# Attention outputs moved by DMA into the transposed layout and scaled on GpSimd, and the row maxima turned by one transpose of 48 columns

## The reference, cut to what matters

```python
# attn_a, causal
attn = where(causal, einsum('bhqd,bhkd->bhqk', q, k) * scale, -inf)
a = clip(attn, -100, 100); m = max(a, -1); e = exp(a - m)
p = e / (sum(e, -1) + 1e-6)
p = p + 1e-8
p = p / sum(p, -1)
out = einsum('bhqk,bhkd->bhqd', p, v)      # then @ w_proj, + x
# ffn, attention part (src is reshaped: 8 batches of 512 rows in this kernel)
probs = softmax(scores, -1)
attn = einsum('bhqk,bkhd->bqhd', probs, v).reshape(B, T, 256) @ Wo + bo
x = layer_norm(src + attn)                 # then the experts
```

## Time and profile before

| | us |
|---|---|
| median of 3 runs | 2586.87 |
| profiled execution | 2582.34 |
| its span | 2580.6 |
| TensorE busy | 2412.5 (93%) |
| VectorE busy | 1835.4 (71%) |
| ScalarE busy | 1436.6 (56%) |
| GpSimd busy | 1353.3 (52%) |

### The profile page before, as it was taken

How to read it: one execution, slowest core, us unless ns; L and a number is a source line. 1 busy time by engine, 2 the same in 40 slices (tenths; PEclk the granted TensorE clock), 3 DMA queues, 4 the chain that set the end, 5 groups by cost and what they waited for, 6 DMA issues and landing times. The chain is left out here.

```text
span 2580.6 us, 45834 instructions
## 1 busy us (share of the span) xinstructions
PE 2412.5 (93%) x14724; PEld 1392.8 (54%) x14724; DVE 1835.4 (71%) x3685; ACT 1436.6 (56%) x2991; POOL 1353.3 (52%) x1358
## 2 busy tenths in 40 slices
PE   5999999999999999989999699988999999989998
PEld 3455555544443444348898366653344444349997
DVE  5999999999778888854333558867778888845333
ACT  3666666666777777753333232214777777753332
POOL 5456666653334455345655579843334444445655
PEclk9999999999999999999999799988999999999999
DMA  5333333433334444325655200015434444335654
GB/s 157 105 106 105 112 98 105 120 102 98 117 109 134 127 130 119 97 92 165 219 194 175 71 1 17 17 58 139 119 108 128 130 129 122 85 119 170 204 197 141
DMA packets 249936, 305.88 MB, mean 119 GB/s; under 512 B 28034, under 2 KB 224865, under 8 KB 249700
## 3 DMA queue, kind: packets, MB, share of 16 engines
q1 hardware_dynamic: 238164, 275.37, 35.6%
q0 software_dynamic: 10176, 26.27, 2.8%
q10 hardware_dynamic: 1360, 1.31, 0.2%
HBM read 210.32 MB, written 92.84 MB: 117 GB/s over the span
## 5 line engine op out<-in xcount | busy, mean ns | idle before, releaser
L773 DVE TENSOR_REDUCE neg_max_af<-sc_af 128x1 f32<-128x512 f32 (+3 forms) x864 | 550.5, 664 | 104.8 <-PE sc_af L479 100.6
L694 ACT ACTIVATE prob_af<-sct_af 128x512 f32<-128x512 f32 (+1 forms) x864 | 484.4, 582 | 243.4 <-PE sct_af L502 239.3
L773 DVE TENSOR_REDUCE neg_max_f<-sc_f 128x1 f32<-128x512 f32 x512 | 334.0, 685 | 91.7 <-PE sc_f L479 89.7
L694 ACT ACTIVATE prob_f<-sct_f 128x512 f32<-128x512 f32 x512 | 291.1, 598 | 135.2 <-PE sct_f L502 133.3
L479 PE MATMUL sc_af<-stack_k_af,stack_q_af 96*128 96x512 bf16 (+3 forms) x1024 | 319.8, 342 | 12.0 <-DVE neg_max_af L773 11.9
L502 PE MATMUL sct_af<-stack_q_af,stack_k_af 99*128 99x512 bf16 (+3 forms) x1024 | 319.8, 343 | 4.1 <-ACT prob_af L694 3.3
L1603 PE MATMUL y_ps_e<-w_r,hT_e 128*128 x1120 | 256.1, 382 | 6.4 <-issue 4.5
L802 DVE SCALAR_TENSOR_TENSOR prob_af<-prob_af,w_r 128x512 f32<-128x512 f32 (+2 forms) x224 | 233.6, 1051 | 20.7 <-ACT prob_af L694 20.6
L530 PE MATMUL out_af<-prob_af,v_aug_af 128*32 128x512 f32 (+3 forms) x2048 | 231.8, 524 | 8.7 <-DVE prob_af L802 7.8
L1790 DVE TENSOR_TENSOR y_e<-y_ps_e,b_e 128x256 f32<-128x256 f32 x70 | 29.7, 425 | 286.4 <-PE y_ps_e L1603 284.5
L1603 PEld LDWEIGHTS y_ps_e<-w_r,hT_e 128*128 128x128 f32 x1120 | 207.2, 190 | 37.3 <-issue 11.3
(11 more groups left out here) (382 smaller groups left out, 4650.1 us busy)
## 6 DMA issues: line engine op xcount, KB each, us to landing
w_r<-in_f_W_dram SPq DMA_DIRECT2D x66, 1024.0 KB, 5.1
stack_k_af<-k_parts_d SPq DMA_DIRECT2D x64, 384.0 KB, 4.2
k_parts_d<-parts_af SPq DMA_DIRECT2D x187, 128.0 KB
q_parts_d<-parts_af SPq DMA_DIRECT2D x96, 128.0 KB
stack_q_af<-q_parts_d SPq DMA_DIRECT2D x64, 192.0 KB, 2.9
stack_k_f<-k_parts_d SPq DMA_DIRECT2D x32, 384.0 KB, 4.2
w_next<-in_f_W_dram SPq DMA_DIRECT2D x12, 1024.0 KB, 5.0
k_parts_d<-parts_f SPq DMA_DIRECT2D x91, 128.0 KB
```

The source lines that it names most:

```text
L694: nc.scalar.activation(dst, src.rearrange("p (h q) -> p h q", h=len(heads)), ACT.Exp).then_inc(S.exp_done, 1)
L773: nc.vector.tensor_reduce(M.neg_max[:, qt, heads[0]:heads[-1] + 1], src, AX.X, ALU.max, negate=True).then_inc(S.max_done, 1)
```

## The change

Outputs of a group stay with heads on partitions. Five transfers of SyncE (`move_out`) take each finished group from `o_sb`: one spreads the 4 rows of sums over 64 partitions of 32 numbers, four move 16 partitions of 512 numbers each to where `attT` wants them. Every two groups (a chunk c of 8 heads) VectorE makes the weights from the sums (`weigh`, 128x32), SyncE stores them to DRAM (`store_weights`) and loads them back spread, each head's row onto 16 partitions (`spread_weights`), and GpSimd scales `attT` (`scale_out`: one operation of 128x512, three for causal). In batches 14, 15, 22 and 23 the second chunk still goes by TensorE (`by_pe`). The maxima are laid out so that one transpose of 48 columns turns all four query tiles. The sum of values is made by two products with one output column each, instead of one with 256. Semaphores of the mean and variance steps are merged; these steps compute and wait as before.

```diff
+    def by_pe(n, c):
+        return c == 1 and n >= NB and n % NB >= NB - 2
...
-        elif kt == 2:
+        elif kt == 2 and by_pe(group(n, g - 1)[0], group(n, g - 1)[1] // 2):
             use = ("out",) + group(n, g - 1)
-        elif s in attT_slots(n):
-            use = ("attT", n - 1, attT_slots(n).index(s))
+        elif s == 3 and exists(n - 1) and by_pe(n - 1, 1):
+            use = ("attT", n - 1, 1)
...
+            def move_out(n, g):
+                if not exists(n) or by_pe(n, g // 2):
+                    return
+                c, h = divmod(g, 2)
+                sp.wait_ge(S.o_sb, NG * n + g + 1)
...
+                sp.dma_start(M.sums[64 * h:64 * h + 64, :], M.o_sb[HD:P:32, :]).then_inc(S.moved, 16)
+                for i in range(4):
+                    o = 64 * h + HD * i
+                    sp.dma_start(M.attT[n % 2][o:o + HD, c, :], M.o_sb[32 * i:32 * i + HD, :]).then_inc(S.moved, 16)
+            def store_weights(n, c):
...
+                sp.wait_ge(S.weighed, chunks(n, c))
+                sp.dma_start(M.weights_d[n % NB][0, hs, :], M.weights[:, 0, :]).then_inc(S.weights_stored, 16)
+                if causal(n):
+                    sp.dma_start(M.weights_d[n % NB][1, hs, :], M.weights[:, 1, :]).then_inc(S.weights_stored, 16)
+            def spread_weights(n, c):
...
+                sp.wait_ge(S.weights_stored, 16 * spreads(n, c))
+                sp.wait_ge(S.moved, 80 * moved(n, 2 * c + 1))
+                if chunks(n, c) > 1:
+                    sp.wait_ge(S.attT_ready, chunks(n, c) - 1)
+                for at in range(2 if causal(n) else 1):
+                    sp.dma_start(M.spread[:, at, :], M.weights_d[n % NB][at, hs, :].unsqueeze(1).to_broadcast([8, HD, T])).then_inc(S.weights_spread, 16)
...
                 load_stack(n, 3)
+                move_out(n - 1, 3)
                 load_max_rows(n, 1)
                 load_res(n - 1)
                 write_parts(n + 1, 0)
+                store_weights(n - 1, 1)
                 load_stack(n + 1, 0)
+                spread_weights(n - 1, 1)
+                move_out(n, 0)
                 load_max_rows(n, 2)
...
-                    for t in range(KT):
-                        last = nc.tensor.transpose(Gb[0:12, t * P:t * P + P], M.max_parts[:, t, :, :].rearrange("p a h -> p (a h)"), C.ident_bf[:, :])
+                    last = nc.tensor.transpose(M.gen_bf[bank_of[use]][0:12 * KT, 0:P], M.max_parts[:, :, :, :].rearrange("p a h t -> p (a h t)"),
+                                               C.ident_bf[:, :])
...
-                if n > 0 or g > 0:
-                    act.wait_ge(S.out_ps, NG * n + g)
+                elif exists(pn):
+                    act.wait_ge(S.moved, 80 * moved(pn, pg))
                 nc.scalar.activation(M.o_sb[:, :], M.out[:, :], ACT.Copy).then_inc(S.o_sb, 1)
...
+            def scale_out(n, c):
...
+                pool.wait_ge(S.weights_spread, 16 * spreads(n, c))
+                out = M.attT[n % 2][:, c, :]
+                if causal(n):
...
+                    nc.gpsimd.tensor_tensor(out, out, M.spread[:, 0, :], ALU.mult).then_inc(S.floor_v, 1)
+                    nc.gpsimd.tensor_scalar(M.spread[:, 1, :], M.spread[:, 1, :], M.v_all[:, n % 2, c:c + 1], None, ALU.mult).then_inc(S.floor_v, 1)
...
+                    nc.gpsimd.tensor_tensor(out, out, M.spread[:, 1, :], ALU.add).then_inc(S.attT_ready, 1)
+                else:
+                    nc.gpsimd.tensor_tensor(out, out, M.spread[:, 0, :], ALU.mult).then_inc(S.attT_ready, 1)
```

More of the change, by code:

```diff
@@ L72, in y_slot, with moved, outs, pe_chunks @@
         return 4 if n == end - 1 else 8
-    def attT_slots(n):
-        return (3, 4) if n == end - 1 else (4, 7)
+    def by_pe(n, c):
+        return c == 1 and n >= NB and n % NB >= NB - 2
+    def moved(n, g):
+        return sum(1 for m in range(n + 1) for q in range(NG) if (m, q) <= (n, g) and not by_pe(m, q // 2))
+    def outs(n, g):
+        return NG * n + g + 1 - moved(n, g)
+    def pe_chunks(n):
+        return outs(n, NG - 1) // 2
+    def chunks(n, c):
+        return moved(n, 2 * c + 1) // 2
+    def spreads(n, c):
+        return chunks(n, c) + min(chunks(n, c), 2 * NB)
     first_ffn = max(first, NB)
@@ L1252, in attention_memory @@
     M.max_rest = sb("max_rest", [P, KT, 4])
[L1253 to L1254 removed]
+    M.max_parts = sb("max_parts", [P, 3, 4, KT], BF16)
+    M.max_sb = sb("max_sb", [12 * KT, 2, P], BF16)
     M.prob = sb("prob", [P, 2, 4, T])
     M.o_sb = sb("o_sb", [P, T])
[L1257 to L1259 removed]
+    M.sums, M.weights = sb("sums", [P, T // HD]), sb("weights", [P, 2, T // HD])
+    M.e8, M.den = sb("e8", [P, T // HD]), sb("den", [P, T // HD])
     M.rden = sb("rden", [P, KT, 4])
[L1261 to L1263 removed]
+    M.spread = sb("spread", [P, 2, T])
+    M.attT = [sb(f"attT{i}", [P, DC, T]) for i in range(2)]
     M.sc = [psum("sc0"), psum("sc1"), psum("sc2")]
```

208 lines of the change are left out of this document (110 added, 98 removed).

## The result

| | before | after |
|---|---|---|
| median, us | 2587.8 (4 runs, 2585.0 to 2590.6) | 2704.2 (4 runs, 2694.8 to 2712.2) |
| profiled execution: time, span | 2582.3, 2580.6 | 2696.4, 2694.7 |
| mean granted clock of TensorE | 0.98 | 0.94 |

The changed kernel is slower: ratio 1.044, 95% interval 1.0415 to 1.0466. The forecast was 2547 us, and the time lies outside the range of 2503 to 2590. It fell on the side of the second rival (rows of the maxima held up by the move), and 70 us beyond its 2634.

The account below looks back on a forecast made before the run. TensorE was taken to bound both the causal and the `ffn` stretches. Matmuls gone 80.6, plus VectorE's relief 8, less floor-row waits 49, made 39.6 us less: 2586.9 - 39.6 = 2547 us, range 2503 to 2590.

Parts of the forecast that it names:

- the second rival: Causal groups: dearer issues and packets queued ahead delay the maxima's rows 2.8 us more in 31 groups; 87 us, 2634 us; chance 0.13.
- the price of the floor rows' waits: Causal batches: TensorE waits 1.1, 1.1, 1.55 and 2.7 us in a batch's four groups; 49 us lost.
- VectorE's relief: Causal stretch: fewer VectorE operations give back 8 of the 20.4 us between TensorE's work, ends 0 and 15.
- that of the third place: Third group of a causal batch: move and load of next x delay the maxima's rows, a wait of 1.55 us.
- the 0.5 us for the new form of the transfer: Maxima's transfer as 48 rows of 256 bytes instead of 12 of 1 KB: 0.5 us more, 2.7 from issue to use.
- the 0.74 beside them: Maxima's transfer if only three engines serve its 48 rows: 0.74 us in place of 0.5, 7 us more in sum.
- Its threshold: Second rival: the floor rows' wait decides against the change from a mean of 89 / 31 = 2.9 us a group.
- The third: Rival, causal groups: only the move's issues are dear, 31 x 1.3 = 40 us; 2587 us, no change; chance 0.10.
- The first: Rival, causal groups: floor rows hardly wait, so 80.6 + 8 = 89 us are gained; 2498 us; chance 0.17.
- TensorE's matmuls in `ffn` batches: The 16 non-causal batches lose transposes of `o_sb`, `att` and maxima from TensorE; 52.0 us gained.
- The fourth rival: `ffn` batches: GpSimd, late through `scale_out`, delays VectorE or ScalarE 2 us in 12 batches; 24 us, 2571 us; chance 0.10.
- the y products did not wait for `scale_out`: Scaling taken as hidden, 3.7 us to spare in a causal batch; first products with `attT` waiting would show the forecast wrong.

Follow-up runs that it names:

- e2: Kernel before, plus five added copies of `o_sb` per causal group, issued by SyncE ahead of the floor rows; 2693.0 us, ratio 1.0385 to before.
- e11: As e2, but two added copies per causal group instead of five; 2615.1 us, ratio 1.0094 to before.
- e1: Changed kernel with the floor rows' transfer issued ahead of `move_out` in all four places of a batch; 2667.8 us, ratio 1.0287 to before.
- e4: Kernel before, plus the same five added copies as e2, but issued behind the floor rows; 2587.0 us, ratio 0.9985 to before.
- e9: Changed kernel without the scaling in `ffn` batches, SyncE instead of GpSimd waiting for the spread there; 2671.2 us, ratio 1.0293 to before.
- e7: Changed kernel, in causal batches only: floor rows ahead of the move, next score rows ahead of weights' store, next floor rows ahead of spread; 2587.3 us, ratio 0.9976 to before.
- e8: e7 with `scale_out(n - 1, 1)` behind `scale_y` in GpSimd's list and `weigh` behind `split_max` on VectorE; 2617.9 us, ratio 1.0085 to before.

## Why the prediction was wrong, step by step

**The step that failed** is the price of the floor rows' waits, "8 x 3.75 + 7 x 2.7 = 49 us". From 60 us to the last product with the output weights the kernel before takes 608 us and the changed one 737. That is 129 us more with 28.6 us of matmuls gone, so the causal batches lost 158 us, where the forecast had 49 for the waits less 8 for VectorE's relief. Two things were wrong in it.

- The larger one: a wait was charged at its own length, and the sum had no term for the clock. Read in pieces of 4 us, the mean clock over these 608 and 737 us is 0.992 and 0.852. With levels of 0.5 and 1 only, TensorE was at the lower one for (1 - 0.852) / 0.5 = 30% of 737 us, 218 us, against 10 before; at half speed the difference is 104 us of work. With 67 us of waits more the estimate is 171, against 158. In the same way e2 gives 58 + 45 = 103 against 96, e11 29 + 11 = 40 against 32, and e1 56 + 28 = 84 against 87 (its 28.6 us of matmuls counted): up to 13 us off, but the same in its parts. e2 and e4 show that the late rows cause it.
- The waits themselves: 67.3 us, mean 2.2 us over 31 groups, where I had 1.6. By places it is less alike. The first two have 12.6 us, where I had 16 x 1.1 = 18; the third has 31.3, where I had 8 x 1.55 = 12; the fourth has 23.4, where I had 7 x 2.7 = 19. So the term that was too small is that of the third place. I had 2.7 us from issue to use everywhere, and the load of x as 0.43 us of issue and nothing more. Measured are 2.3 us with the move alone ahead (2.8 in two waits and 3.3 in one, each with a spread or score rows issued some 5 us before), 3.7 to 4.8 behind the load of x, and 2.9 to 4.8 behind the store. The issues were dearer too: a block's has a median of 0.59 us, where I had 0.43 by an issue of another shape; four take 2.5 us in most groups and up to 3.4, so the move is 3.1 to 4.0 us and not 2.55. Against that, the 0.5 us for the new form of the transfer were too much, and so were the 0.74 beside them: it shows as 0.1.

**The rivals.** The second came nearest and had the right side: rows held up by dearer issues and by packets queued ahead. But it priced the waits at 49 + 87 = 136 us, twice the 67 measured, and had no clock either; that its 2634 us is nearer to 2704 than mine is in part luck. Its threshold, a mean wait of 2.9 us, was wrong for the reason above: the change was already a loss at 2.2. The third had issues dearer by 1.3 us a group; they were dearer by 0.6 in most and by 1.4 at most. The first was excluded by 27 waits.

**TensorE's matmuls in `ffn` batches**, 52 us: they are gone, and 24 us came of it. Starts of the maxima's transpose and of the next product, which answer to the last of the earlier trace rows:

```profile
960.83 0.24 PE L508 MATMUL gen_af<-ident_bf,max_parts_af 128*48 128x128 bf16 x1
961.00 0.39 PE L574 MATMUL sct_af<-stack_q_af,stack_k_af 99*128 99x512 bf16 x1
```

0.17 us where it was 0.32: this is also the median of 45 such places. The four had a part that does not shrink with their number: the one transpose holds TensorE for 0.17 and not 0.08, so it saves 0.15 and not 0.24, 9 us less over 96 groups (6 of them in `ffn` batches). 15.6 us went to waits for `neg_max`, and by e9 the scaling costs 16 us; these two overlap, since e9 brings 10.5 of the 15.6 back. Counted once, they and the 6 us make 27 of the 28, closer than single executions can vouch for. The fourth rival priced a late GpSimd at 24 us, near in size; the rows show VectorE's casts beside GpSimd's long instructions as its path.

**VectorE's relief**, 8 us: not seen. With no floor row late (e7) TensorE waits 38 us for `prob` and `max_parts`, against 7.8 before. `weigh` stands ahead of `split_max` in slot kt = 3, and I had counted its operations but not what waits behind them. Moving it back did not help as such: in e8 the waits for `max_parts` went and others took their place.

**What held:** the transposes left TensorE, the y products did not wait for `scale_out`, GpSimd's waits for the spread (186 us in the causal batches, 165 and 164 in the two calls' `ffn` batches) did not reach TensorE directly, the floor rows waited.

The 9 us after the last product of the second call stay unexplained; the other kernels here have 274 to 284 us to the end. I did not look for the cause.

## What to carry to other kernels

A queue that issues transfers is an engine with a critical path: before work is put into it, list what stands behind it and when that is needed, in issues and in bytes; the same five transfers cost some 105 us in front of a short urgent one and nothing behind it. Work put in front also pushes what stood there before, here a load of 512 KB, up against the urgent transfer. Where TensorE is at its upper clock nearly all the time, the waits here cost about twice their length in sum, though not each of them; read the granted clock beside the busy share. An order that is right in one kind of batch (rows first where the floor needs them) can be wrong in the other, so try it for each kind apart.

## What the runs showed of the hardware

- After single stalls of 1.67 to 3.78 us TensorE was granted 1.2 GHz for 12 to 17 us in the stretch shown, busy throughout. After five stalls of 0.80 to 0.84 us and one of 1.62 it kept 2.4 GHz for at least 12 us. Waits of 12.1, 45.5 and 67.3 us for the rows went with mean clocks of 0.94, 0.90 and 0.83 over 60 to 636 us. In e7 a fall of some 7 us came with a wait for VectorE of 2.20 us that ended at 364.29.
- Transfers from SBUF to SBUF cost SyncE 0.59 us of issue at the median for 16 rows of 2 KB (up to 1.47), 0.6 for the four rows of sums, 0.82 for the rows of the maxima.
- A 12 KB transfer that TensorE waited for was used 2.2 to 2.4 us after its issue in most places where no load or store stood right ahead of it in the queue, 3.6 to 4.8 us right behind a load of 512 KB, 2.8 to 4.8 right behind a store of 512 KB, and 6.0 to 6.9 us within 4 us of 1.25 MB (e1).
- VectorE's casts of 16 elements a partition lasted until the GpSimd instruction beside them ended, up to 2.05 us in place of 0.19 in the place shown.
- One transpose of 48 columns held TensorE 0.17 us from start to start, four of 12 columns 0.32.
